# Scan layer of a one-core Perceiver kernel: value and weight projections a step sooner, softplus in two pieces

## The chip, the cores and the metric

The kernel runs on one core of a Trainium2 chip. Times are device microseconds (us). A program has one instruction queue for each engine: TensorE (PE in the profile), VectorE (DVE), ScalarE (ACT), GpSimd (POOL) and SyncE (SP, which issues DMAs here). An engine takes its instructions in the order in which they are written; between engines the order is kept by semaphores, which one instruction raises when it is done and another waits for.

## What is computed

Six layers run one after the other on tokens of shape (16, 64, 512): a cosine cross layer, self-attention, a layer of experts, cross-attention, a decayed attention, and a feed-forward layer. The change is in the fifth, the decayed attention. Its reference, cut to what matters:

```python
q = (x @ W_q.T).reshape(Bx, Sx, H, DH)          # Bx 16, Sx 64, H 8, DH 64
k = (x @ W_k.T).reshape(Bx, Sx, H, DH)
v = x @ W_v.T
b = (q * k).sum(-1) * SCALE
alpha = (x @ W_alpha_w.T + W_alpha_b).reshape(Bx, Sx, H, DH)
a = -jax.nn.softplus(alpha).sum(-1)
...
def step(carry, inp):                            # 63 times, one after the other
    ln, nm, sg = carry
    a_t, b_t, vl_t, vs_t = inp
    ln = _stable_lse(a_t + ln, b_t)
    dec = a_t[..., None] + nm
    new = b_t[..., None] + vl_t[:, None, :]
    m = jnp.maximum(dec, new)
    ssum = sg * jnp.exp(dec - m) + vs_t[:, None, :] * jnp.exp(new - m)
    ...
```

followed by the product of the outputs with `W_o`.

## The kernel before

The layer holds (batch, head) on the 128 partitions and the 512 columns of a token's value in the free dimension, and walks over 64 tokens: eight groups `c` of eight steps `j`, `t = 8 c + j`. Each engine's queue is written out by hand as the same double loop, and each has a schedule of extra work at given `j`, which prepares the next group `c + 1` (or `c + 2`).

The recurrence of a step, on DVE: `s` (line 2043, two halves), `ep` (2058, a maximum with ACT's `ear` and `ebv`), `sg` (2074) and the new state (2080, written into `rb`, a part of W0, which the profile calls W). Extra DVE work stands either between `s` and `ep`, or between `ep` and `sg`. On ACT, step `t` is `ear` (1903, two halves, from the state of step `t - 1`), then `scaled(t + 1)` (`bv`, 1889, and `ebv`, 1893, from a PSUM bank that PE filled), then the extra work of that `j`. On PE, step `t` is `values(t + 2)` (1756, two matmuls that pick token rows), then the extra work of that `j`, then `head_sums(t)` (1768, eight records of 16 columns, from the new state).

The extra work of a group, in the order in which it needs itself:

- PE `project(c, w)` (twelve matmuls of 512 columns at line 116): V (values), A (weights of the decay; it begins with the bias, line 1734), Q and K. V and Q share the bank `ps[0]`: Q waits until `take_v` has read V. A has `ps[1]`, K `ps[2]`.
- ACT `take_v` (1837), then DVE `make_v`, ACT `first_v` (1842), DVE `rest_v` (1952).
- ACT `take_a`: Abs (1846), Exp (1848) and Ln (1851, with a load of its function table before it), then DVE `softplus` (1957, 1959).
- ACT `take_q` (1856), then DVE `products` (1965, 1967, 1971: query times key from PSUM, sums by head, the spread over heads), then PE `by_head` (1748), DVE `by_head` and `logs`, ACT `exponents` (with a table load back), DVE `weights`.
- ACT `take_y(c)` (1866): reads the eight `head_sums` of a finished group out of PSUM. It stands in step 0 of the next group, ahead of `take_v`, and waits for the last of them. PE `out_proj(c - 1)` (1778), step 5, and DVE `add_out`, step 7, follow from it. Group 0 has no `out_proj` in it.

Before the loop the same pieces are written out once for group 0, and V of group 1 is projected there, ahead of the first two `values`.

Of the kernel before, what the change touches and what calls it, by code (L numbers as in the profile page):

```python
# [1634 lines left out]
def decayed_attention_layer(nc, a, e):  # L1635

    x, cn, ps, ones, ident, sem, W0 = e.x, e.cn, e.ps, e.ones, e.ident, e.sem, e.W0
    W5_Q, W5_K, W5_V, W5_A, W5_O = range(5)
# [3 lines left out]
    NG = S // G  # L1642
    VB, RB, AHEAD = 2, 4, 2
    HALVES = slice(0, D // 2), slice(D // 2, D)
    with ExitStack() as st:
# [46 lines left out]
        with nc.Block() as block:  # L1692
# [29 lines left out]
            @block.tensor  # L1722
            def _(pe):
                def project(c, w):

                    pe.wait_ge(ln.xT_ready, BASE + c + 1)
                    pe.wait_ge(w_lo, BASE + ORDER.index(w) + 1)
                    if w == W5_V:
                        bank, done = ps[0], v_mm
                        pe.wait_ge(q_sb, BASE + c)  # L1730
                    elif w == W5_A:
                        bank, done = ps[1], a_mm
                        pe.wait_ge(a_used, BASE + c)
                        nc.tensor.matmul(bank, ones[0:1, :], bal[0:1, :], start=True, stop=False)
                    elif w == W5_Q:
                        bank, done = ps[0], q_mm
                        pe.wait_ge(v_sb, BASE + c + 1)
                    else:
                        bank, done = ps[2], k_mm
                        pe.wait_ge(own_sb, BASE + c)  # L1740
                    split_product(nc, bank, lambda part, k: xT[c % 2][part][:, k, :],
                                  lambda part, k: ws[part][:, ORDER.index(w), k, :], DK, w != W5_A).then_inc(done, 1)

                def by_head(c):

                    pe.wait_ge(spread_sb, BASE + c + 1)
                    pe.wait_ge(k_used, BASE + c + 1)
                    nc.tensor.matmul(ps[2][:, 0:P], same, spread[:, :, :].rearrange("p j e -> p (j e)"),
                                     start=True, stop=True).then_inc(same_mm, 1)

                def values(t):

                    pe.wait_ge(v_lo, BASE + t // G + 1)
                    pe.wait_ge(ebv_sb, BASE + t + 1)
                    for part in range(2):
                        mm = nc.tensor.matmul(ps[4 + t % VB], pick[:, t % G * P:(t % G + 1) * P],
                                              vs[part][:, t // G % 2, :], start=(part == 0), stop=(part == 1))
                    mm.then_inc(vb_mm, 1)

                def head_sums(t):  # L1760

                    c, j = divmod(t, G)
                    if j == 0:
                        pe.wait_ge(yT_sb, BASE + c + 1)
                    for k in range(DK):
                        pe.wait_ge(r_sb, BASE + 2 * t + 3 + 2 * k // DK)
                        col = k * G * B + j * B
                        mm = nc.tensor.matmul(ps[6 + c % 2][:, col:col + B], rb[:, t % RB, k * P:(k + 1) * P], sel,  # L1768
                                              start=True, stop=True)
                    mm.then_inc(y_mm, 1)  # L1770

                def out_proj(c):

                    pe.wait_ge(yT_sb, BASE + 2 + c + 1)
                    pe.wait_ge(ln.xT_ready, BASE + min(c + 4, NG))
                    pe.wait_ge(z_used, BASE + c)
                    for k in range(DK):
                        mm = nc.tensor.matmul(ps[3], yT[:, c % 2, k, :], wo[:, k, :], start=(k == 0), stop=(k == DK - 1))
                    mm.then_inc(z_mm, 1)

                def turn_x(c):

                    pe.wait_ge(z_used, BASE + max(c - 3, 0))
                    ln.tensor(pe, c)

                pe.sem_inc(y_mm, RB)
                pe.wait_ge(s_bal, BASE + 16)
                turn_x(0)
                for w in ORDER:
                    project(0, w)  # L1790
                turn_x(1)
                pe.wait_ge(s_apart, BASE + 16)
                by_head(0)
                project(1, W5_V)
                pe.wait_ge(pick_sb, BASE + 1)
                for t in range(AHEAD):
                    values(t)
                pe.wait_ge(s_wo, BASE + 16)
                for c in range(NG):
                    for j in range(G):  # L1800
                        t = G * c + j
                        if t + AHEAD < S:
                            values(t + AHEAD)
                        if j == 0 and c + 1 < NG:
                            project(c + 1, W5_A)
                        elif j == 1 and c + 1 < NG:
                            project(c + 1, W5_Q)
                        elif j == 2 and c + 1 < NG:
                            project(c + 1, W5_K)
                        elif j == 3 and c + 2 < NG:  # L1810
                            turn_x(c + 2)
                        elif j == 4 and c + 1 < NG:
                            by_head(c + 1)
                        elif j == 5 and c >= 1:
                            out_proj(c - 1)
                        elif j == 7 and c + 2 < NG:
                            project(c + 2, W5_V)
                        head_sums(t)
                out_proj(NG - 1)

            @block.scalar
            def _(act):
# [21 lines left out]
                def take_a(c):  # L1844
                    act.wait_ge(a_mm, BASE + c + 1)
                    nc.scalar.activation(mag, ps[1], ACT.Abs).then_inc(mag_sb, 1)
                    act.wait_ge(mag_sb, BASE + c + 1)
                    nc.scalar.activation(mag, mag, ACT.Exp, scale=-1.0).then_inc(ex_sb, 1)
                    act.wait_ge(ex_sb, BASE + c + 1)
                    act.wait_ge(a_used, BASE + c)  # L1850
                    nc.scalar.activation(lg, mag, ACT.Ln, bias=cn[:, CN_ONE:CN_ONE + 1]).then_inc(lg_sb, 1)
# [24 lines left out]
                first_w(3)  # L1876
                take_v(0)
                take_a(0)
                take_q(0)
                first_v(0)  # L1880
                act.wait_ge(s_pick, BASE + 16)
# [15 lines left out]
                for c in range(NG):  # L1897
                    for j in range(G):
                        t = G * c + j
                        for h, cols in enumerate(HALVES):  # L1900
                            act.wait_ge(r_sb, BASE + 2 * t + h + 1)
                            act.sem_inc(seen)
                            nc.scalar.activation(ear[:, cols], rb[:, (t - 1) % RB, cols], ACT.Abs,
                                                 scale=eal[:, t:t + 1]).then_inc(ear_sb, 1)
                        if t + 1 < S:
                            scaled(t + 1)
                        if j == 0:
                            if c >= 1:
                                take_y(c - 1)
                            if c + 1 < NG:  # L1910
                                take_v(c + 1)
                        elif j == 1 and c + 1 < NG:
                            take_a(c + 1)
                        elif j == 2 and c + 1 < NG:
                            take_q(c + 1)
                        elif j == 3 and c + 1 < NG:
                            first_v(c + 1)
                        elif j == 4 and c + 2 < NG:
                            turned_x(c + 2)
                        elif j == 6 and c + 1 < NG:  # L1920
                            exponents(c + 1)
# [3 lines left out]
            def _(ve):  # L1925
# [110 lines left out]
                for c in range(NG):  # L2036
                    for j in range(G):
# [7 lines left out]
                        if j == 0 and c + 2 < NG:  # L2045
                            stats(c + 2)
                        elif j == 3 and c + 1 < NG:
                            products(c + 1)
                        elif j == 4 and c + 1 < NG:
                            rest_v(c + 1)  # L2050
                        elif j == 5 and c + 2 < NG:
                            turned_x(c + 2)
                        elif j == 7 and c + 1 < NG:
                            weights(c + 1)
# [6 lines left out]
                            ln.vector_norm(ve, c + 2)  # L2061
                        if j == 1 and c + 1 < NG:
                            make_v(c + 1)
                        elif j == 2 and c + 1 < NG:
                            softplus(c + 1)
                        elif j == 5 and c + 1 < NG:
                            by_head(c + 1)
                            logs(c + 1)
# [462 lines left out]
```

## Time and profile before

| | |
|---|---|
| median of 3 runs | 2100.69 us (2099.38 to 2103.79) |
| profiled execution, its own time | 2103.43 us |
| its span | 2101.6 us |
| busy PE, DVE, ACT | 1909.5 (91%), 1361.1 (65%), 1137.4 us (54%) |
| the scan, from the first `s` to the last | 1601.9 to 1866.0 us of the span |

The profile is one execution. Busy shares are means over six layers with different limits; what the change is worth is read from the stretch of the scan. An idle time ahead of an instruction is written with what ended it.

### The profile page before, as it was taken

The page shows a single profiled execution, that of the slowest core. Times are in us where ns is not written, and L with a number is a line of the kernel's source. Part 1 is how long each engine was busy: PE and PEld are TensorE (multiplying, and loading weights), DVE is VectorE, ACT ScalarE, POOL GpSimd, SP SyncE. Part 2 cuts the span into 40 slices and gives each one's busy share as a digit, 9 for nine tenths or more (in the row PEclk, how much of TensorE's full clock was granted, in tenths as well). Part 3 has the DMA queues.
Part 4 walks back from the last instruction along what each step waited for, and adds up shares of the span by engine and source line. Part 5 has one row for each costly group of instructions (what it writes and reads, how often), then busy time and mean ns, then how long its engine had stood idle before and what let it go on. Part 6 is the DMA issues. An engine that isn't in the chain of part 4 may idle for free. (4 is left out here: it accounts for less than half of the span.)

```text
span 2101.6 us, 31827 instructions
## 1 busy us (share of the span) xinstructions
PE 1909.5 (91%) x10570; PEld 1522.1 (72%) x10570; DVE 1361.1 (65%) x2477; ACT 1137.4 (54%) x1878; POOL 136.7 (7%) x136
## 2 busy tenths in 40 slices
PE   7988886799999489999999999999968989889998
PEld 5656775799999377787878787878756767665664
DVE  4755663799999255445463636363637899887686
ACT  5753321688888144445454545444526667657663
POOL 0000000111111111000000000000000000002121
PEclk9998995899999799999999999999998888879999
DMA  6200005234441521100000001010213000020000
GB/s 236 97 31 1 0 0 222 73 148 169 176 156 34 208 77 46 51 30 35 30 35 30 35 30 35 30 35 30 80 50 128 1 1 1 1 86 1 0 20 20
DMA packets 22744, 129.68 MB, mean 62 GB/s; under 512 B 3602, under 2 KB 3858, under 8 KB 18963
## 3 DMA queue, kind: packets, MB, share of 16 engines
q1 hardware_dynamic: 17714, 112.59, 14.5%
q0 software_dynamic: 4960, 16.26, 2.3%
q8 instruction: 33, 0.54, 0.1%
q14 instruction: 37, 0.30, 0.0%
HBM read 116.51 MB, written 12.32 MB: 61 GB/s over the span
## 5 line engine op out<-in xcount | busy, mean ns | idle before, releaser
L116 PE MATMUL PS<-cT,qs 128*128 128x512 f32 x1152 | 300.4, 406 | 2.5 <-DVE qs L1538 2.2
L116 PE MATMUL PS<-pT,cN 128*128 128x512 f32 x1152 | 270.2, 392 | 2.0 <-DVE pT L1538 2.0
L116 PEld LDWEIGHTS PS<-cT,qs 128*128 128x128 f32 x1152 | 210.7, 189 | 52.2 <-issue 8.0
L116 PEld LDWEIGHTS PS<-pT,cN 128*128 128x128 f32 x1152 | 213.9, 188 | 45.7 <-DVE pT L1538 2.2
L116 PE MATMUL PS<-fw,xgT 128*128 128x384 f32 x1104 | 204.6, 340 | 5.7 <-DVE xgT L1080 5.7
L116 PEld LDWEIGHTS PS<-fw,xgT 128*128 128x128 f32 x1104 | 192.8, 190 | 9.9 <-DVE xgT L1080 6.3
L1533 DVE TENSOR_REDUCE nmax<-PS 128x1 f32<-128x512 f32 x128 | 87.7, 685 | 162.7 <-PE PS L116 162.5
L116 PE MATMUL PS<-ws,xT 128*128 128x512 f32 x672 | 183.1, 431 | 6.4 <-DVE ws L560 4.9
L1080 DVE TENSOR_TENSOR fw<-W,fw 128x1536 fp32r<-128x1536 f32 x92 | 159.4, 1755 | 24.2 <-ACT fw L1003 24.2
L116 PEld LDWEIGHTS PS<-ws,xT 128*128 128x128 f32 x672 | 139.3, 210 | 46.4 <-issue 11.3
L1438 ACT ACTIVATE qp<-PS 128x512 f32<-128x512 f32 x96 | 57.5, 599 | 190.0 <-PE PS L116 190.0
L1003 ACT ACTIVATE fw<-W 128x1536 fp32r x92 | 134.4, 1489 | 34.6 <-issue 34.6
L1538 DVE TENSOR_TENSOR pT<-PS,pT 128x512 fp32r<-128x512 f32 x128 | 87.0, 685 | 53.2 <-ACT pT L1460 53.2
L1460 ACT ACTIVATE pT<-PS 128x512 fp32r<-128x512 f32 x128 | 75.5, 597 | 80.9 <-PE PS L1333 80.8
L2191 PE MATMUL PS<-W,hs 128*128 128x512 f32 x256 | 114.6, 593 | 0.0
L116 PE MATMUL PS<-xT,ws 128*128 128x512 f32 x384 | 106.1, 427 | 6.4 <-DVE ws L2325 5.0
L977 PE MATMUL PS<-pw,hT 128*128 128x512 f32 x414 | 102.8, 403 | 4.7 <-DVE hT L1080 4.7
L1768 PEld LDWEIGHTS PS<-cn,W 128*128 128x128 f32 x512 | 78.1, 225 | 39.4 <-DVE W L2080 32.5
L1443 ACT ACTIVATE pb<-PS,nmax 128x512 f32<-128x512 f32 x128 | 87.5, 684 | 29.8 <-DVE nmax L1533 29.7
L149 POOL TENSOR_TENSOR rs<-ve,cn 128x1 f32<-128x1 f32 x33 | 19.1, 579 | 1231.7 <-DVE ve L144 1231.7
L1768 PE MATMUL PS<-cn,W 128*128 128x16 f32 x512 | 76.7, 284 | 24.4 <-DVE W L2080 24.3
L116 PEld LDWEIGHTS PS<-xT,ws 128*128 128x128 f32 x384 | 73.7, 193 | 34.2 <-issue 12.4
(266 smaller groups left out, 3442.3 us busy)
## 6 DMA issues: line engine op xcount, KB each, us to landing
W<-in_fc SPq DMA_DIRECT2D x8, 3072.0 KB, 11.0
cT<-in_ctxT SPq DMA_DIRECT2D x16, 768.0 KB, 4.3
raw_pj<-in_proj SPq DMA_DIRECT2D x8, 1536.0 KB, 6.6
ct_in<-in_ctxT SPq DMA_DIRECT2D x16, 768.0 KB, 4.4
cn_in<-in_ctxN SPq DMA_DIRECT2D x16, 768.0 KB, 5.3
W<-in_w SPq DMA_DIRECT2D x2, 4096.0 KB, 12.9
routed_y<-y POOLq DMA_DIRECT2D x23, 256.0 KB
W<-in_w SPq DMA_DIRECT2D x5, 1024.0 KB, 7.4
```

The source lines that it names most:

```text
L116: mm = nc.tensor.matmul(out, lhs(m, s), rhs(n, s), start=(opens and (s, m, n) == terms[0]), stop=((s, m, n) == terms[-1]))
L149: self.nc.gpsimd.tensor_tensor(self.rs[:, :], self.ve[:, :], self.cn[:, CN_MHALF:CN_MHALF + 1], ALU.pow).then_inc(self.rstd, 1)
L977: mm = nc.tensor.matmul(ps[7], hT[m][:, f, :], pw[n][:, f, :], start=(f == 0 and m == n), stop=(f == FK - 1 and m == 1))
L1003: nc.scalar.activation(fw[0][:, :, fc_cols(c)], raw_fc_of(par, c), ACT.Copy).then_inc(fc_hi, 1)
L1080: return nc.vector.tensor_tensor(out, whole, first.bitcast(F32), ALU.subtract)
L1438: nc.scalar.activation(out, src, ACT.Copy, scale=scale).then_inc(w_sb, count)
L1443: nc.scalar.activation(pb[:, g % 2, :], ps[g % 2], ACT.Exp, bias=nmax[:, g % 4:g % 4 + 1], accum_out=rsum[:, g % 4:g % 4 + 1]).then_inc(e_ ...
L1460: nc.scalar.activation(turned(pT[0], g), ps[2 + g % 2].rearrange("p (j n) -> p j n", j=JK), ACT.Copy).then_inc(pt_hi, 1)
L1533: nc.vector.tensor_reduce(nmax[:, g % 4:g % 4 + 1], ps[g % 2], AX.X, ALU.max, negate=True).then_inc(m_dve, 1)
L1538: return nc.vector.tensor_tensor(out, whole, first.bitcast(F32), ALU.subtract)
L1768: mm = nc.tensor.matmul(ps[6 + c % 2][:, col:col + B], rb[:, t % RB, k * P:(k + 1) * P], sel, start=True, stop=True)
L2191: mm = nc.tensor.matmul(ps[HB + t], hs[:, n % HR, t * P:(t + 1) * P], w26[:, f, :], start=(f == 0), stop=(f == FT - 1))
```

## The change

In PE's loop A of the next group goes from `j == 0` to `j == 7` of the group before, and V from `j == 7` to `j == 6`. A of group 1 is projected before the loop. On ACT the logarithm is taken out of `take_a` into `take_log`, a step later, and `take_q` goes from step 2 to step 3. On DVE `softplus` goes from step 2 (after `ep`) to step 3 (before `ep`), `products` from step 3 to step 4 (before `ep`), and `rest_v` in step 4 from before `ep` to after it.

```diff
@@ PE, ahead of the loop
                 by_head(0)
                 project(1, W5_V)
+                project(1, W5_A)
                 pe.wait_ge(pick_sb, BASE + 1)
@@ PE, the loop
-                        if j == 0 and c + 1 < NG:
-                            project(c + 1, W5_A)
-                        elif j == 1 and c + 1 < NG:
+                        if j == 1 and c + 1 < NG:
                             project(c + 1, W5_Q)
...
+                        elif j == 6 and c + 2 < NG:
+                            project(c + 2, W5_V)
                         elif j == 7 and c + 2 < NG:
-                            project(c + 2, W5_V)
+                            project(c + 2, W5_A)
                         head_sums(t)
@@ ACT
                     nc.scalar.activation(mag, mag, ACT.Exp, scale=-1.0).then_inc(ex_sb, 1)
+
+                def take_log(c):
                     act.wait_ge(ex_sb, BASE + c + 1)
                     act.wait_ge(a_used, BASE + c)
                     nc.scalar.activation(lg, mag, ACT.Ln, bias=cn[:, CN_ONE:CN_ONE + 1]).then_inc(lg_sb, 1)
...
                 take_a(0)
+                take_log(0)
                 take_q(0)
...
                         elif j == 2 and c + 1 < NG:
+                            take_log(c + 1)
+                        elif j == 3 and c + 1 < NG:
                             take_q(c + 1)
-                        elif j == 3 and c + 1 < NG:
                             first_v(c + 1)
@@ DVE, between s and ep
                         elif j == 3 and c + 1 < NG:
+                            softplus(c + 1)
+                        elif j == 4 and c + 1 < NG:
                             products(c + 1)
-                        elif j == 4 and c + 1 < NG:
-                            rest_v(c + 1)
@@ DVE, between ep and sg
-                        elif j == 2 and c + 1 < NG:
-                            softplus(c + 1)
+                        elif j == 4 and c + 1 < NG:
+                            rest_v(c + 1)
```

## Rows read from the trace of the kernel before

**Rows 1.** The page's first line: the span.
```profile
span 2101.6 us, 31827 instructions
```

**Rows 2.** Windows: length; busy PE, PEld, DVE, ACT, POOL; granted clock; DMA share, GB/s.
```profile
1659.00:1665.00 6.00, 4.66 (x14) 3.44 (x14) 5.86 (x20) 2.60 (x6) 0.00 (x0) 0.50 0.00 0
1666.00:1673.00 7.00, 7.00 (x37) 5.38 (x36) 6.79 (x24) 5.14 (x10) 0.00 (x0) 1.00 0.00 1
1673.00:1706.00 33.00, 29.65 (x142) 22.61 (x141) 31.39 (x90) 23.73 (x44) 0.68 (x1) 0.90 0.00 1
```

**Rows 3.** Groups by line over the scan layer: busy us, mean ns; idle before.
```profile
L2058 DVE TENSOR_TENSOR ep<-ear,ebv 128x256 f32<-128x256 f32 x128 | 48.6, 423 | 15.2 <-ACT ear L1903 15.2
...
L1965 DVE TENSOR_TENSOR W<-W,PS 128x512 f32<-128x512 f32 x8 | 5.5, 688 | 2.6 <-PE PS L116 2.5
...
L1856 ACT ACTIVATE W<-PS 128x512 f32<-128x512 f32 x8 | 4.7, 586 | 0.0
```

**Rows 4.** Timeline, all engines, steps 0 to 2 of group 1: start, duration, us.
```profile
1637.94 0.96 PE L1768 MATMUL PS<-cn,W 128*128 128x16 f32 x8
...
1638.94 1.14 ACT L1866 ACTIVATE yT<-PS 128x512 f32<-128x512 f32 x1 [2.56 <-PE PS L1768]
...
1640.99 0.76 DVE L2058 TENSOR_TENSOR ep<-ear,ebv 128x256 f32<-128x256 f32 x2 [1.71 <-ACT ear L1903]
...
1646.36 1.28 ACT L1851 ACT_TABLE_LOAD   x1
1647.66 0.72 ACT L1851 ACTIVATE W<-W,cn 128x512 f32<-128x512 f32 x1
...
1648.88 0.76 DVE L2058 TENSOR_TENSOR ep<-ear,ebv 128x256 f32<-128x256 f32 x2 [3.48 <-ACT ear L1903]
```

**Rows 5.** Timeline of DVE: end of group 1, group 2, start of group 6.
```profile
1665.19 0.88 DVE L2043 SCALAR_TENSOR_TENSOR s<-W,al,bv 128x256 f32<-128x256 f32 x2
...
1672.76 0.88 DVE L2043 SCALAR_TENSOR_TENSOR s<-W,al,bv 128x256 f32<-128x256 f32 x2
...
1676.72 0.88 DVE L2043 SCALAR_TENSOR_TENSOR s<-W,al,bv 128x256 f32<-128x256 f32 x2
1677.51 0.76 DVE L2058 TENSOR_TENSOR ep<-ear,ebv 128x256 f32<-128x256 f32 x2
...
1812.90 0.88 DVE L2043 SCALAR_TENSOR_TENSOR s<-W,al,bv 128x256 f32<-128x256 f32 x2
...
1815.70 0.89 DVE L2043 SCALAR_TENSOR_TENSOR s<-W,al,bv 128x256 f32<-128x256 f32 x2
```

**Rows 6.** Timeline of PE: groups 0, 1 and 5; then of ACT, group 2.
```profile
1632.83 5.28 PE L116 MATMUL PS<-ws,xT 128*128 128x512 f32 x12
...
1667.58 0.96 PE L1768 MATMUL PS<-cn,W 128*128 128x16 f32 x8
...
1668.93 0.96 PE L1768 MATMUL PS<-cn,W 128*128 128x16 f32 x8
...
1670.29 2.96 PE L116 MATMUL PS<-ws,xT 128*128 128x512 f32 x12
1673.08 0.96 PE L1768 MATMUL PS<-cn,W 128*128 128x16 f32 x8
...
1674.53 1.12 PE L1734 MATMUL PS<-bal,cn 1*128 1x512 f32 x2
...
1678.49 0.96 PE L1768 MATMUL PS<-cn,W 128*128 128x16 f32 x8
...
1807.56 0.96 PE L1768 MATMUL PS<-cn,W 128*128 128x16 f32 x8
...
1674.02 0.67 ACT L1893 ACTIVATE ebv<-PS,ebe 128x512 f32<-128x512 f32 x1
```

**Rows 7.** Timeline of ACT and DVE: the first step of the scan.
```profile
1601.22 0.69 ACT L1889 ACTIVATE bv<-PS,be 128x512 f32<-128x512 f32 x1 [3.56 <-issue]
...
1601.94 0.88 DVE L2043 SCALAR_TENSOR_TENSOR s<-W,al,bv 128x256 f32<-128x256 f32 x2 [2.70 <-ACT bv L1889]
```

## The prediction, on record before the result

> **What bounds the kernel now.** I read the page first: the span is 2101.6 us [rows 1], and the scan that the change touches is one stage of it. Then the windows of one group of the scan: DVE is busy 31.4 of 33 us and PE 29.7 in group 2 (groups are counted from 0, steps within a group too) [rows 2]. So DVE sets the pace, PE is not far behind it, and what a group loses it loses to waits. The list of groups by line says which: in the whole scan DVE stood before `ep` for 15.2 us until ACT had made `ear`, and 2.6 us before `products` for the key product of PE [rows 3]. The rest of the DVE time between two steps is work, and the change leaves all of that work on DVE; it only re-orders it.
>
> The timelines show where the 15.2 us arise. In group 1 of the scan, `take_y` starts at 1638.94 after ACT idled 2.56 us for the `head_sums` of the last step of group 0, `take_v` and `ear` follow it, and `ep` of step 1 comes at 1640.99 after 1.71 us of idling [rows 4]. Then `take_a` waits for PE's weight product, the table load and the logarithm follow it (1646.36, 1647.66), `ear` of step 2 is last in that queue, and `ep` of step 2 stands 3.48 us [rows 4]. These two mechanisms are the argument: the second is what the change takes away, the first is what it feeds.
>
> **What is removed.** With the weight product (call it A) done a step before the group starts, `take_a` in step 1 waits for nothing, and with the logarithm in step 2 it is no longer ahead of `ear` of step 2. I take away all 15.2 us before `ep`, and the 2.6 before `products`, since these move to step 4, while the key product stays at step 2. Together -17.8 us.
>
> **What is added inside a group.** (a) The logarithm. In step 2 ACT now ends `ebv` 1.93 us after DVE's `s` (1674.02 + 0.67 against 1672.76, [rows 5, 6]), then loads the table for 1.28, and the logarithm takes 0.72 [rows 4], so that `lg` is there about 3.98 us after that `s`. DVE's step 2 has nothing extra now and lasts 2.80 (1812.90 to 1815.70, [rows 5]); `softplus` stands behind `s` of step 3, ready 0.79 later (1676.72 to 1677.51, [rows 5]), at 3.56. Wait 0.42 us, seven groups: +2.9. The Trainium skill ("ScalarE: Activation LUTs", What ACT_TABLE_LOAD costs) gives 2.66 us for a switch of tables, a drain included; by that the wait would be 1.38 longer and the sum 9.7 us higher. The trace has the logarithm 1.30 us after the load's start [rows 4], so the row decides.
> (b) The other DVE pieces (`products`, `rest_v`, `softplus`) change steps; they ran between DVE instructions with no gap and do so again. Cost nothing, as DVE is the pace either way. `take_q` (0.59, [rows 3]) and `first_v`, of the same size, now stand together in step 3 of ACT: its `ear` begins 1.1 us after DVE's `s`, `ear` and the two of `scaled` take about 2.0 (as above, with the 0.1 by which `ear` starts before `s`), so all is done at 4.3, and DVE's step 3 lasts 2.80 + 1.3 (`softplus`) + 0.42 = 4.5. The cover is 0.2 us; if it is gone, `ear` of step 4 is late by the rest. No DMA moves and SP's and POOL's queues are not passed.
> (c) PE. This is the costly part. The output projection in step 5 of group 1 keeps PE until 1667.58, though DVE is in step 6 since 1665.19 [rows 5, 6]; PE then owes `head_sums` and `values` (1.35 us, to 1668.93), the same again (to 1670.29), the value product V (2.79, to 1673.08), and only then `head_sums` of step 7 [rows 6]. Now V stands in step 6 and A in step 7, each ahead of that step's `head_sums`. A with its bias costs 3.96 us (1674.53 to 1678.49, [rows 6]). So `head_sums` of step 7 starts at 1667.58 + 1.35 + 2.79 + 1.35 + 3.96 = 1677.03, not 1673.08. Behind it on ACT stands `take_y` in step 0, which waits for it, and behind `take_y`, `take_v`, and `ear` of step 1. `take_y` can start 1.00 us after that `head_sums` (1637.94 to 1638.94, [rows 4]): 1678.03, 10.45 us after the projection's end. `ep` follows `take_y` by 2.05 (1640.99 - 1638.94, [rows 4]): 1680.08. DVE is ready for it at 1677.51 [rows 5]. Wait: 2.57 us. In general the wait is 10.45 + the projection's end - the start of step 0 - 2.70.
> So for the five groups whose predecessor has a projection, groups 2 to 6: the last is group 6, 3.57 us (1807.56 and 1812.90; its step 0 has no statistics and DVE comes 1.16 sooner, so 1.54 stands for 2.70) [rows 5, 6], the three between give 2.8, 3.8 and 3.4. Sum of the five 16.2. Group 1 comes after a group without a projection, but PE runs V at half speed there (5.28 us, [rows 6]): V can start 2.8 us sooner, and A adds 3.96; `take_y` is later than before by 0.2 us with V at full speed, and by 2.5 with V at half. I take the middle, 1.3, on top of the 1.8 it waited: 3.1. So +19.3 us.
>
> **Before the scan.** A of group 1 is now put ahead of the first `values`. ACT's `bv`, which reads them, starts at 1601.22 after 3.56 us of idling, and DVE's first `s` at 1601.94 after 2.70 [rows 7]. Nothing else is late there, so the scan starts later by the whole of A: +4.0 (the bounds: little over nothing, if ACT's idle before `bv`, which the trace puts down to issue, is not PE's doing; 6.3 with A's twelve matmuls at half speed, as V's 5.28 against 2.96 [rows 6]).
>
> **Sum.** -17.8 + 2.9 + 19.3 + 4.0 = +8.4 us. The profiled execution took 2103.43 us for its 2101.6 us of span, 2.7 above the median of the three runs, 2100.69; it would become 2111.8, and the median 2109.1. That is 0.4%; 0.2% (4 us) is about what can be told from no change here.
>
> **The clock is the unknown.** PE's granted clock was 0.50, the lower level (1.2 GHz), while DVE was in step 5, and 1.00 after PE had been busy with the projection [rows 2]. The Trainium skill ("TensorE: Matmul & The Clock Gate", HAM oscillation) says that matmuls put next to each other keep the clock up while idle gaps lower it. The change does both: V and A come together, steps 3 and 4 on PE get thinner. If the clock stayed up through step 5, PE would be done with the projection before DVE's step 6 begins (1665.19, [rows 5]), and its `head_sums` would start there and not at 1667.58.
>
> **Rivals.**
> *R1, faster: the clock stays at the upper level through steps 4 and 5.* The term "projection's end" then becomes the start of step 6, 1665.19: 2.4 us sooner in group 2's case, which leaves 0.2 of its 2.57; the other four shrink to 0.2, 0.2, 0.2 and 1.3, group 1's to 0.6. That is 2.7 for 19.3, so the sum is 16.6 lower: -8.2, 2092.5. It decides from the point where the six waits are 1.4 us shorter each. Against it: PE idles more, not less, in steps 3 and 4, where `by_head` now waits for `products` of the later step.
> *R2, slower still: the lower clock reaches into V.* V would cost 5.1 instead of 2.79, +2.3 in five groups and +1.2 in group 1: 12.7 more, 2121.8. For it: V ran at half in group 0 [rows 6]; against it, in the later groups the projection has always brought the clock back.
> *R3, no difference:* A is partly hidden, before the scan by an idle that was not PE's (-4.0), and the waits are a little shorter than worked out. Then 2105 and below, to 2100.
> *R4: the change does not do what it says,* as `softplus` stays late in step 3 because ACT is behind from step 1 on. One load and logarithm late (1.28 + 0.72) in each of seven groups is 14.0 more, 2123. Against it: DVE's own wait in step 1 delays both engines alike, and ACT's `take_a` (two instructions) ends well before DVE's norm and `make_v` do.
>
> **Numbers.** The forecast as it stands (2105 to 2114) 0.63; R1 0.08; R2 0.12; R3 0.12, a sixth of it on the faster side and a tenth on the slower; R4 0.05. So faster 0.10, same 0.10, slower 0.80. The range 2101 to 2117 leaves out R1 and the upper parts of R2 and R4.
>
> **What would show it.** `take_y` idles for `head_sums` in six groups, some 3 to 4 us each, and `ep` of step 1 idles about 19 us in all; `ep` of step 2 not at all, and step 2 lasts 2.8; `softplus` idles 0.4 after the logarithm, seven times; `products` never waits for PE. The first `s` comes 4 us later. I am wrong if `take_y` finds its sums ready, that is if PE has caught up by step 7, or if the lower clock moves.

## The result, and the profile after

The changed kernel takes 2111.32 us in the median of six runs (2106.34 to 2113.11), the kernel before, on the same chip, 2100.18 (2098.86 to 2103.79). The ratio is 1.0049, 95% interval 1.0036 to 1.0063: slower by 11.1 us, where 8.4 was forecast. The profiled execution took 2110.7 us, its span is 2108.9.

The two profiled spans differ by 7.3 us only, because in this execution the layers ahead of the scan were about 3 us quicker: PE's first `by_head` started at 1592.2 instead of 1595.5. From there to the start of the last `head_sums` record the changed kernel takes 286.0 us, the one before 275.2 (both end points are in PE's rows of lines 1748 and 1768): +10.7 before rounding. I use this stretch, "the scan" below, beside the medians; it is read from one execution of each kernel, and can differ from the medians by some us.

The groups by line over the scan layer (busy us, mean ns, idle us ahead of it and its releaser), against [rows 3] and [rows 7]:

```profile
L1869 ACT ACTIVATE yT<-PS 128x512 f32<-128x512 f32 x8 | 8.9, 1112 | 26.8 <-PE PS L1768 26.8
...
L2048 DVE SCALAR_TENSOR_TENSOR s<-W,al,bv 128x256 f32<-128x256 f32 x128 | 55.9, 477 | 6.7 <-ACT bv L1893 6.7
L2063 DVE TENSOR_TENSOR ep<-ear,ebv 128x256 f32<-128x256 f32 x128 | 48.2, 418 | 22.6 <-ACT ear L1907 22.6
...
L1962 DVE SCALAR_TENSOR_TENSOR W<-PS,W 128x512 f32<-128x512 f32 x8 | 5.5, 692 | 6.0 <-ACT W L1854 6.0
...
L1970 DVE TENSOR_TENSOR W<-W,PS 128x512 f32<-128x512 f32 x8 | 5.4, 679 | 0.4 <-PE PS L116 0.4
```

Four idle times of DVE changed: before `ep` 22.6 us instead of 15.2, before `products` 0.4 instead of 2.6, before the first `s` 6.7 instead of 2.7, and before `softplus` 6.0 instead of 3.6 (3.8 and 3.6 of these lie ahead of the loop). In the list of waits over the same stretch, which gives the number of waits and the longest, all of `ep`'s lie in six places, and `softplus` has seven of 0.3 us in the scan:

```profile
ACT yT L1869 <- PE PS L1768: 26.8, 7, 5.1
DVE ep L2063 <- ACT ear L1907: 22.6, 6, 5.5
...
DVE W L1962 <- ACT W L1854: 2.2, 7, 0.3
```

The timeline of the turn from group 1 to group 2, PE first, against [rows 6]:

```profile
1663.69 4.56 PE L1778 MATMUL PS<-W,yT 128*128 128x512 f32 x8
1668.09 0.96 PE L1768 MATMUL PS<-cn,W 128*128 128x16 f32 x8
...
1669.44 2.96 PE L116 MATMUL PS<-ws,xT 128*128 128x512 f32 x12
1672.24 0.96 PE L1768 MATMUL PS<-cn,W 128*128 128x16 f32 x8
...
1673.69 1.12 PE L1734 MATMUL PS<-bal,cn 1*128 1x512 f32 x2
1674.74 3.07 PE L116 MATMUL PS<-ws,xT 128*128 128x512 f32 x12
1677.65 0.96 PE L1768 MATMUL PS<-cn,W 128*128 128x16 f32 x8
```

```profile
1678.64 1.11 ACT L1869 ACTIVATE yT<-PS 128x512 f32<-128x512 f32 x1 [3.33 <-PE PS L1768]
1679.54 0.65 ACT L1838 ACTIVATE v<-PS 128x512 f32<-128x512 f32 x1
1680.07 0.90 ACT L1907 ACTIVATE ear<-W,eal 128x256 f32<-128x256 f32 x2
...
1686.16 1.28 ACT L1854 ACT_TABLE_LOAD   x1
1687.46 0.72 ACT L1854 ACTIVATE W<-W,cn 128x512 f32<-128x512 f32 x1
```

```profile
1680.68 0.76 DVE L2063 TENSOR_TENSOR ep<-ear,ebv 128x256 f32<-128x256 f32 x2 [2.46 <-ACT ear L1907]
...
1688.21 0.69 DVE L1962 SCALAR_TENSOR_TENSOR W<-PS,W 128x512 f32<-128x512 f32 x1 [0.32 <-ACT W L1854]
```

Read down: projection, V, A, and only then the sums of step 7 (1677.65); `take_y` stands 3.33 us for them, `ear` is behind it, and `ep` stands 2.46. The forecast put 2.57 there. Step 2 of this group then has no wait, and `softplus` waits 0.32 in step 3.

Group 1 is the worst place. PE and DVE there:

```profile
1630.46 4.98 PE L116 MATMUL PS<-ws,xT 128*128 128x512 f32 x12
...
1637.77 4.61 PE L116 MATMUL PS<-ws,xT 128*128 128x512 f32 x12
```

```profile
1645.25 0.76 DVE L2063 TENSOR_TENSOR ep<-ear,ebv 128x256 f32<-128x256 f32 x2 [5.54 <-ACT ear L1907]
```

V runs at the lower clock nearly throughout (4.98 us against 2.96; the mean granted clock over it is 0.54) and A in part (4.61 against 3.07; 0.61).

### The profile page after: what moved, and what is told of

The parts are those of the page before. It is cut to its first block and busy times, and to the rows that moved or that the text cites. A ratio compares the mean times of both kernels' runs of the same rounds, so it can differ in the third digit from the quotient of the medians.

```text
span 2108.9 us, 31827 instructions
## 1 busy us (share of the span) xinstructions
PE 1906.7 (90%) x10570; PEld 1514.9 (72%) x10570; DVE 1360.4 (65%) x2477; ACT 1136.9 (54%) x1878; POOL 136.8 (6%) x136
## 5 line engine op out<-in xcount | busy, mean ns | idle before, releaser
L1443 ACT ACTIVATE pb<-PS,nmax 128x512 f32<-128x512 f32 x128 | 87.5, 684 | 29.8 <-DVE nmax L1533 29.7
```

What stands on the lines that cost most here:

```text
L1443: nc.scalar.activation(pb[:, g % 2, :], ps[g % 2], ACT.Exp, bias=nmax[:, g % 4:g % 4 + 1], accum_out=rsum[:, g % 4:g % 4 + 1]).then_inc(e_ ...
```

## The experiments

Each ran beside the kernel before on its chip. "Ratio" is to that kernel, with its 95% interval; "scan" is the stretch defined above in the profiled execution; the last two columns are DVE's idle time before `ep` and ACT's before `take_y`, in the scan layer.

| kernel | median us | ratio | scan us | `ep` idle | `take_y` idle |
|---|---|---|---|---|---|
| before | 2100.18 | 1 | 275.2 | 15.2 | 7.9 |
| changed | 2111.32 | 1.0049 (1.0036 to 1.0063) | 286.0 | 22.6 | 26.8 |
| e1 A of group 1 in the loop | 2107.58 | 1.0039 (1.0025 to 1.0053) | 282.1 | 22.4 | 26.6 |
| e2 ACT's and DVE's part alone | 2092.87 | 0.9969 (0.9958 to 0.9980) | 266.5 | 6.0 | 5.3 |
| e3 `take_y` in step 1 | 2102.53 | 1.0008 (0.9996 to 1.0019) | 275.4 | 8.5 | 4.6 |
| e4 sums ahead of A | 2099.86 | 1.0003 (0.9993 to 1.0014) | 272.0 | 5.9 | 4.2 |
| e5 as e2, V in step 6 | 2091.83 | 0.9951 (0.9938 to 0.9964) | 266.2 | 6.6 | 3.5 |
| e6 changed, fillers | 2107.99 | 1.0032 (1.0019 to 1.0044) | 282.8 | 19.6 | 24.6 |
| e7 as e2, fillers | 2089.88 | 0.9946 (0.9933 to 0.9959) | 261.6 | 1.5 | 5.9 |
| e8 changed, A twice | 2139.21 | 1.0180 (1.0165 to 1.0195) | 313.3 | 50.0 | 51.3 |
| e9 changed, more fillers | 2100.22 | 1.0004 (0.9993 to 1.0014) | 271.9 | 8.4 | 16.5 |
| e10 as e7, fillers at both ends | 2086.09 | 0.9939 (0.9926 to 0.9952) | 260.4 | 1.2 | 4.1 |
| e11 before, fillers | 2097.79 | 0.9995 (0.9983 to 1.0007) | 268.8 | 9.4 | 5.4 |
| e12 PE's part alone | 2117.38 | 1.0086 (1.0073 to 1.0100) | 288.9 | 26.4 | 26.1 |

### The two halves of the change

**e2_split_only**: PE's queue of the kernel before, ACT's and DVE's of the changed one.

```diff
@@ against the changed kernel, PE
-                project(1, W5_A)          # ahead of the loop
...
-                        if j == 1 and c + 1 < NG:
+                        if j == 0 and c + 1 < NG:
+                            project(c + 1, W5_A)
+                        elif j == 1 and c + 1 < NG:
...
-                        elif j == 6 and c + 2 < NG:
-                            project(c + 2, W5_V)
                         elif j == 7 and c + 2 < NG:
-                            project(c + 2, W5_A)
+                            project(c + 2, W5_V)
```

> The kernel before, with ACT's and DVE's part of the change alone; all of PE's queue is as before (V in step 7, A in step 0, nothing new ahead of the loop). Queue theory (the loss is all PE's new order, and what ACT's and DVE's new order brings was paid away there): take_y waits as before (some 3 us in all), A is as late as before, but load and logarithm (2.0 us) no longer stand ahead of ear of step 2, so that of the 13.4 us of idling before ep in step 2 about 4 are left; softplus idles 2.2 us, products saves 2.2. About 9 us less than before, 2091 us. Rival (softplus, products and rest_v in their new steps cost time themselves): not below before, 2100 or more.

Measured: 2092.87, 6.9 us less than the kernel before, and 8.7 less in the scan. `ep` idles 6.0 us. The half that splits `softplus` is a gain by itself; the rival, that the new steps of `softplus`, `products` and `rest_v` cost time, falls. I expected 2 us more. Two idle times are longer than expected: `softplus` idles 7.8 us (3.8 of it ahead of the loop) and not 5.8, and `ep` of step 2 5.3 us and not 4. A is late there (in groups 2 to 6 its twelve matmuls took 4.6 us, not 3.07, in part at the lower clock) and pushes the whole of `take_a` and the logarithm behind it.

**e12_pe_only**: the other half, the same diff the other way, on the kernel before.

> The kernel before with PE's part of the change alone (V in step 6, A in step 7, A of group 1 ahead of the loop); ACT and DVE as before, with the logarithm in take_a and softplus in step 2. If the two halves add up: PE's half costs the start (4.0 us) and the idling before ep of step 1 (22.6 us), and takes away the wait of take_a for A and of products for K, but the logarithm (2.0 us) still stands ahead of ear of step 2, which then idles about 1 us in each of seven groups (7 us instead of 13.4): about 2100 + 4 + 21 - 6 - 2 = 2117 us, 6 us more than the changed kernel. If ACT's and DVE's half brought nothing once PE's is in: 2111 us.

Measured 2117.38, the 2117 of the sum; `ep` idles 26.4 us in 13 places. In the medians the two halves add: +17.9 us for PE's, -6.9 for the other, +11.0 together, and the change measured +11.1. In the profiled scans they don't: +13.7 and -8.7 make +5.0, where the changed kernel has +10.7. Each scan is one execution, so that each half has its sign, but how nearly they are independent stays open.

### What is behind PE's half

**e1_bias_in_loop** takes back the product ahead of the loop alone.

```diff
                 project(1, W5_V)
-                project(1, W5_A)
...
-                        if j == 1 and c + 1 < NG:
+                        if t == 0:
+                            project(1, W5_A)
+                        elif j == 1 and c + 1 < NG:
```

> The changed kernel, with group 1's weight product A back in step 0 of group 0 instead of ahead of the first values. Start theory (the first step waited for the whole of A, 4.0 us): the first s idles 2.7 us instead of 6.7, nothing else gets later, because take_a of group 1 now has its logarithm a step later; 3.9 us less than the changed kernel, about 2107.4 us. Rival (the 4 us are given back within group 0, for instance as a wait of take_a for A and of ep for ear): no difference to the changed kernel, 2111.

Measured 2107.58, 7.8 us over its kernel before where the changed one is 11.1 over, and a scan 3.9 us shorter than the changed kernel's; the first `s` idles as before:

```profile
1600.30 0.88 DVE L2049 SCALAR_TENSOR_TENSOR s<-W,al,bv 128x256 f32<-128x256 f32 x2 [2.71 <-ACT bv L1894]
```

So 3.9 us of the loss in the scan (3.3 in the medians) are the start, though the trace of before put ACT's idle there down to issue.

**e4_sums_first** swaps one pair in PE's queue.

```diff
-                        elif j == 7 and c + 2 < NG:
-                            project(c + 2, W5_A)
                         head_sums(t)
+                        if j == 7 and c + 2 < NG:
+                            project(c + 2, W5_A)
```

> The changed kernel, with head_sums of step 7 put ahead of A in PE's queue; same instructions, one pair swapped. Queue theory: take_y finds its sums as early as in the kernel before (idle 3 us in all instead of 26.8), ep of step 1 idles 2 us instead of 22.6; A, 4 us later by one head_sums, is still long ahead of take_a; about 20 us less than the changed kernel, 2091 us. Rival (clock): PE's low stretches, not the order, make it late, and the time stays within 5 us of 2111. Second rival (A behind the sums makes values of step 1 and bv late instead): half of the 20 us comes back as idling before s of step 1, 2101.

Measured 2099.86: 0.1 us from its kernel before where the changed one is 11.1 over, and a scan of 272.0 against 286.0. `take_y` idles 4.2 us instead of 26.8, and steps 1 of groups 2 to 5 last 4.3 us, without a wait. But I expected 20 us, and got 11 in the medians and 14 in the scan: the second rival comes in with a third to a half. The timelines of PE and of ACT, steps 1 and 2 of group 3:

```profile
1706.66 1.12 PE L1734 MATMUL PS<-bal,cn 1*128 1x512 f32 x2
1707.71 4.61 PE L116 MATMUL PS<-ws,xT 128*128 128x512 f32 x12
1712.16 0.63 PE L1756 MATMUL PS<-vs,pick 128*128 128x512 f32 x2
```

```profile
1709.68 0.91 ACT L1907 ACTIVATE ear<-W,eal 128x256 f32<-128x256 f32 x2 [0.42 <-DVE W L2085]
1712.88 0.69 ACT L1893 ACTIVATE bv<-PS,be 128x512 f32<-128x512 f32 x1 [2.29 <-issue]
...
1714.67 0.63 ACT L1849 ACTIVATE W<-W 128x512 f32<-128x512 f32 x1
1715.21 0.89 ACT L1907 ACTIVATE ear<-W,eal 128x256 f32<-128x256 f32 x2
```

`bv` stands 2.29 us: its `values` are now the first thing behind A in PE's queue, and it starts 0.09 us after their end. `take_a` follows later and pushes `ear` of step 2. The place of the wait was not quite the rival's (`ep` of step 2 and `softplus`, not `s`). The clock has a share too: A took 4.6 us in groups 2 to 6 here, against 3.07 in the changed kernel, which is 1.54 of the 2.29 us.

**e3_take_y_later** leaves PE alone and moves the waiting instruction.

```diff
@@ ACT, j == 0
-                            if c >= 1:
-                                take_y(c - 1)
@@ ACT, j == 1
                                 take_a(c + 1)
+                            if c >= 1:
+                                take_y(c - 1)
```

> The changed kernel, with ACT's take_y moved from step 0 to step 1, behind take_a; PE's and DVE's queues are those of the changed kernel. Queue theory: when take_y comes up, the sums are there in all groups but the first; ep of step 1 idles near 0 instead of 22.6 us in groups 2 to 6; ACT's step 1 (ear, scaled, take_a, take_y, some 4.3 us) just fits DVE's 4.3; group 1 keeps some 2 us. 20 us less than the changed kernel, about 2091 us. Rival (clock: PE is late because its clock is lower, and everything that needs PE is late wherever ACT's wait stands): the idling moves to take_y in step 1 or to bv, and the time stays within 5 us of 2111.

Measured 2102.53; scan 275.4, 10.6 us shorter than the changed kernel's. The queue theory's idling before `ep` in step 1 is gone but for group 1, the clock rival's figure (within 5 us of 2111) is not met; the size is again about half. With `take_y` out of the way it is `bv`, behind A (22.2 us of idling in ten places, 7.6 of it before the first step), that makes ACT's full step 1 overrun.

**e8_a_twice** doubles the suspected cost: A is computed twice, the first result overwritten.

```diff
+                            project(c + 2, W5_A, False)   # signals nothing
                             project(c + 2, W5_A)
```

> The changed kernel with A computed twice in a row in step 7 (six groups). Queue theory: each further 3.96 us ahead of the last head_sums goes in full into take_y and into ep of step 1; 6 x 3.96 = 23.8 us more, 2135 us, and 46 us of idling before ep instead of 22.6. Rival (the wait of take_y has something else at its end, or PE has gaps to take it up): clearly less than 20 us more.

Measured 27.9 us more than the changed kernel (scan +27.3), a little over the 23.8. Each microsecond of PE ahead of those sums goes into the time; PE has no gap that takes it up. The excess is traced too: a further A put off what follows it by 4.05 us, 24.3 in six groups, and the projections of groups 1 to 5 took 29.8 us together instead of 26.7, for the lower clock; that makes 27.4, and `ep` idles 27.4 us more.

**e5_values_early** tells which of PE's two moved products matters.

```diff
@@ against e2_split_only
-                        elif j == 7 and c + 2 < NG:
+                        elif j == 6 and c + 2 < NG:
                             project(c + 2, W5_V)
```

> The kernel e2_split_only (2092.9 us) with V in step 6 instead of step 7; A stays in step 0. Queue theory: V stands ahead of the last head_sums either way and PE has no gap between steps 6 and 7 of groups 1 to 5, so that these sums, and take_y, come at the same time: 2093 us, within 2. Rival (V's move has its own share in the loss of the changed kernel): 2 to 6 us more than e2_split_only, with idling before take_y.

Measured 2091.83, scan 266.2 against 266.5. The idle before `ep` lies in other places (2.5 us of it in step 2 of group 1), but its sum and the time are the same: with A in step 0, V's move costs nothing that shows. What PE's half costs is A's move.

### The clock

**e6_clock_kept** puts matmuls whose results nobody uses into PE's gaps of steps 3 and 4 of the changed kernel, to keep its activity up.

```diff
+                def filler(c, n):
+                    pe.wait_ge(yT_sb, BASE + c + 2)
+                    for k in range(n):
+                        nc.tensor.matmul(ps[6 + (c + 1) % 2], xT[(c + 1) % 2][0][:, k % DK, :],
+                                         ws[0][:, 0, k % DK, :], start=True, stop=True)
...
                             turn_x(c + 2)
+                            filler(c, 5)
                         elif j == 4 and c + 1 < NG:
+                            filler(c, 6)
                             by_head(c + 1)
```

> The changed kernel with 5 and 6 matmuls of 512 columns put into PE's gaps of steps 3 and 4 (results unused, in a bank that is free then). Clock theory (a part of the 22.6 us before ep of step 1 is the projection at the lower clock): the granted clock stays at 2.4 GHz through step 5, the projection takes 3.5 to 4 us instead of 4.6 to 6.1, the waits of groups 2 to 6 get 1 to 2 us shorter each, 8 to 12 us in all: 2099 to 2103 us. Queue order alone (the clock does not matter, or does not stay up for so few matmuls): 2111 us, or more by what the fillers cost.

Measured 2107.99, scan 3.2 us shorter: less than the clock theory asked for, and the interval of its ratio overlaps that of the changed kernel. But the clock had not been kept; the projection still took 4.7 to 6.0 us. **e9_clock_held** uses 5, 8 and 10 of them in steps 2, 3 and 4.

> The changed kernel with more fillers than e6_clock_kept (5 matmuls in step 2, 8 in step 3, 10 in step 4), which left lower-clock stretches of 3 to 7 us in step 5 and projections of 4.7 to 6.0 us. Clock theory: with the clock held at 2.4 GHz through steps 3 to 5, as it was in e7_split_clock_kept (projection 3.6 us), the idling before ep of step 1 falls from 22.6 to 5 to 9 us, and the time from 2111 to 2094 to 2098. If the clock were not the cause of e6's small gain: 2108 or more.

Measured 2100.22, scan 271.9. Windows of it over step 5 of group 1 and on (the columns of [rows 2]), and PE's timeline:

```profile
1657.00:1663.00 6.00, 6.00 (x30) 3.95 (x28) 5.86 (x20) 3.41 (x8) 0.00 (x0) 1.00 0.00 0
1664.00:1671.00 7.00, 7.00 (x28) 4.90 (x27) 6.64 (x22) 5.15 (x11) 0.00 (x0) 0.86 0.00 1
```

```profile
1658.79 3.60 PE L1778 MATMUL PS<-W,yT 128*128 128x512 f32 x8
1662.22 0.96 PE L1768 MATMUL PS<-cn,W 128*128 128x16 f32 x8
```

With the granted clock at 1.00 (2.4 GHz) the projection takes 3.60 us, and `ep` idles 8.4 us instead of 22.6. So 11 of the changed kernel's microseconds hang on the lower clock. Of the 14.2 us that `ep` idles less, 4.8 are group 1's, which has no projection before it: there V and A took 2.97 and 3.07 us instead of 4.98 and 4.61. The other 9.4 are those of groups 2 to 6, where the projection ends sooner. Neither theory alone holds the whole: with the clock up, `take_y` still idles 16.5 us for sums behind A. The fall of `ep`'s idling is in the expected range, the time is 2 us above it.

The clock was not held everywhere. The second window has a mean of 0.86 although PE is busy in all of its 7 us: from 1670 to 1672 the granted clock was 0.50, and A took 4.60 us in group 2's case and 4.61 in group 6's, instead of 3.07. These are the two groups whose `ep` still idles 2.3 and 3.3 us.

**e7_split_clock_kept** is e2_split_only with the fillers of e6.

> The kernel e2_split_only with the same fillers. Clock theory: PE is through with the projection 1 to 2 us sooner, A and with it take_a come sooner, and the idling before ep of step 2 (6.0 us in all) goes to about 1: 2088 us. Without an effect of the clock: 2093 us or more.

Measured 2089.88, scan 261.6 (4.9 us shorter than that of e2_split_only), `ep` idles 1.5 us. The median is 3.0 us lower, but the intervals of the two ratios just overlap. Here the few fillers kept the clock over the projection; the six projections in groups 1 to 6 take 3.6 to 3.7 us each:

```profile
1657.70 3.60 PE L1778 MATMUL PS<-W,yT 128*128 128x512 f32 x8
1661.13 0.96 PE L1768 MATMUL PS<-cn,W 128*128 128x16 f32 x8
1661.94 0.71 PE L1756 MATMUL PS<-vs,pick 128*128 128x512 f32 x2
1663.23 1.06 PE L1768 MATMUL PS<-cn,W 128*128 128x16 f32 x8 [0.58 <-DVE W L2093]
```

PE now waits for DVE again in step 6, it owes nothing. **e10_split_clock_ends** adds `filler(c, 6)` in steps 5 and 6 of group 0 and `filler(c, 5)` in the last group, in all steps but 5.

> The kernel e7_split_clock_kept (2089.9 us) with fillers in steps 5 and 6 of group 0 and in the last group as well. Clock theory: V in group 0 takes 3.0 instead of 5 us, so that step 1 of group 1 idles no more (0.5 us); in the last group the projection and the one after the last step (5.7 and 5.4 us) take 3.6 each, the second with nothing to hide it: 2 to 3 us less, 2087.5. Rival (fillers delay head_sums or values where PE has no gap): 2090 or more.

Measured 2086.09, the best of the study, 1.2 us in the scan from e7. Group 1 idles no more in step 1 (4.32 us long). The projections did not all gain: in the last group 3.6 us instead of 5.7, but 5.4 in two groups in the middle, and the one after the last step takes 6.7 instead of 5.4. Its difference to e7 (3.8 us in the medians) is in the direction expected, but the intervals of the two ratios overlap; against e2_split_only, without fillers, they don't (0.9952 at most against 0.9958 at least).

**e11_before_clock_kept** puts e6's fillers into the kernel before.

> The kernel before with the fillers of e7_split_clock_kept and nothing else. Clock theory: part of its 15.2 us of idling before ep is A at the lower clock (4.6 instead of 3.1 us in groups 1, 3 and 5) behind a slow projection; with the clock kept, steps 2 last about 4.7 us as in group 2, and the idling falls to 4 to 6 us: about 10 us less, 2090 us. Order alone: no change, 2100.

Measured 2097.79, ratio 0.9995 (0.9983 to 1.0007), runs from 2092.27 to 2105.1: not told apart from no change, though its profiled scan is 6.4 us shorter and `ep` idles 9.4 us. I expected 10 us; what the fillers cost or gain elsewhere is open.

## Why the prediction was right

Point by point, by its own terms (measured ones from the groups by line above and the waits):

| term | forecast | measured |
|---|---|---|
| `ep` and `products`, waits taken away | -17.8 | -17.4 (15.2, and 2.2 of 2.6) |
| `softplus` waits for the logarithm | +2.9 | +2.4 (6.0 against 3.6) |
| `ep` of step 1, behind `take_y` | +19.3 | +22.6 |
| start of the scan | +4.0 | +4.0 (6.7 against 2.7) |
| sum | +8.4 | +11.6; scan +10.7, medians +11.1 |

**What is removed.** Right: no wait before `ep` in step 2 is left, and step 2 lasts 2.80 us in all groups. The 0.4 us of `products` that stayed belong to group 0, ahead of the loop, which the change doesn't touch.

The terms measured add up to 0.9 us more than the scan grew; that rest is not assigned.

**(a) The logarithm.** The mechanism is right, the wait 0.3 us and not 0.42 (the parts named there, 1.93, 1.30 and 0.72, make 3.95 and not 3.98). The table load and the logarithm start 1.30 us apart (1686.16, 1687.46), as in [rows 4]; no drain of 1.38 us stands there. The figure of the Trainium skill ("ScalarE: Activation LUTs", What ACT_TABLE_LOAD costs) would have put 9.7 us on the sum, which the run does not show.

**(b)** Nothing, as said: from the first `s` to the last `head_sums` DVE is busy 245.4 us, and was 245.7 before, and e2 is faster with the pieces in their new steps.

**(c) PE.** The chain of reasons held link by link: projection, V, A, sums, `take_y`, `ear`, `ep`; e4 and e3 cut it at two places, e8 doubled one link, and e5 showed that V, which stood ahead of the same sums before, adds nothing by its move. The mis-sized part is group 1: 3.1 us forecast, 5.54 measured. I took the middle between V at full and at half speed; V ran at half, and A, costed at full, took 1.54 us more as well. The same A took 4.61 us in the kernel before too (from 1640.44), so that this could have been costed.

Groups 2 to 6 were forecast at 16.2 us and make 17.0. The general formula holds almost exactly: with the changed kernel's own ends of the projection and starts of step 0 it gives 2.45, 3.46, 3.96, 2.48 and 4.60 us, where `ep` idles 2.46, 3.49, 3.98, 2.50 and 4.61. In e9 it gives 0.73, 0.69, 0.66, 0.62 and 1.76, where `ep` idles 2.27, 0.74, 0.71, 0.67 and 3.29; the two that are off are the groups in which A took 1.54 us more. So the ends of the projection were the unknown. Its five durations were 4.67, 4.94, 6.01, 5.61 and 4.64 us before and 4.56, 5.61, 6.13, 4.70 and 5.68 in the changed kernel: the clock moved them from group to group, and that their sum moved by 0.8 us only is luck for a forecast that took them over from the trace of before.

**R1, the clock.** Rightly refused as the likeliest: the windows of the changed kernel read a granted clock of 0.50 over steps 4 and 5 of group 1, as in [rows 2]:

```profile
1659.00:1665.00 6.00, 4.45 (x14) 3.32 (x14) 5.86 (x19) 2.06 (x4) 0.00 (x0) 0.50 0.00 0
1666.00:1673.00 7.00, 7.00 (x36) 5.18 (x34) 6.79 (x23) 5.39 (x11) 0.00 (x0) 1.00 0.00 1
```

As a conditional figure it had the direction and most of the size of the waits, not the time: e9, whose clock stays up through steps 4 and 5, idles 14.2 us less before `ep`, where R1 took off 16.6; but it ends at no difference to the kernel before, where R1 gave -8.2. Its waits are about 0.7 us in groups 1 and 3 to 5, where I had 0.2 to 0.6, and 2.3 and 3.3 us in groups 2 and 6, where I had 0.2 and 1.3. The rule of the Trainium skill ("TensorE: Matmul & The Clock Gate", HAM oscillation), that gaps lower the clock and closed-up work keeps it, is borne out in part: in e7 and e9 the clock stayed up through step 5 with the gaps ahead of it filled. Against it stand the groups 2 and 6 of e9, where it fell under A though PE had no gap. Putting V next to A did not keep the clock: it had fallen ahead of the projection.

**R2** came true in group 1 alone. **R3** fell with e1: the idle before the first `bv` is PE's. **R4** fell with the rows of step 3.

What I had not worked out: that taking A from the front of `head_sums` leaves it in front of `values`. The forecast needed only the first wait behind A, and the second was hidden behind it, until e3 and e4 took the first away. In e3, where A took 3.07 us in groups 2 to 6 as in the changed kernel, this second wait gave back about half of what I expected. In e4 A at the lower clock made it longer.

## What to carry to other kernels

An engine with spare time on the average can be without any in the stretch that counts: in the kernel before PE idled 25 of the 269 us of the steps, but between step 5 and step 0 it is behind, and a product added there moves everything queued after it. Before work is moved earlier, find what stands behind its new place in the queue, and who waits for that; a semaphore wait in the middle of another engine's queue (here `take_y`) passes the delay to work that has nothing to do with it. And test the halves of a compound change apart: one half gained 6.9 us, the other lost 17.9.

## What the runs showed of the hardware that was not expected

Unused matmuls made a kernel faster, clear of the noise in e9 against the changed kernel (1.0004 against 1.0049). They took `ep`'s idling from 22.6 to 8.4 us, and the projection from between 4.6 and 6.1 us to 3.60, with a granted clock of 1.00 over it instead of 0.50. How many are wanted could not be told beforehand: 5 and 6 matmuls in steps 3 and 4 kept the clock over the projection in e7, and did not in e6, where the projections still took 4.7 to 6.0 us.

A PE without gaps can lose the clock. In e9 it is busy in all of the window from 1664 to 1671, and the granted clock falls from 1.00 to 0.50 in it; in e4 A took 4.61 us right behind other matmuls. Which of PE's work the clock answers to was not tested.

An idle put down to "issue" was a wait for another engine where it was tested: ACT before the first `bv` idles 3.56 us in [rows 7], and 7.6 with A ahead of `values`. For `bv` behind A in e4 (2.29 us) the times of the rows say the same, but no run took that A away.

The layers ahead of the scan varied by some 4 us between the profiled executions without any change to them: the first `by_head` of the scan started between 1591.5 (e2) and 1595.9 us (e7).
